# Fourteen matmuls on stored weights per turn, in front of six TensorE stages of a fused transformer kernel

## The reference, cut to what matters

```python
h = h + _L0_attn_ref(_layernorm(h), ...)   # 12 heads of 16, quantised q, k, v, weights; no softmax
h = h + _L0_ffn_ref(_layernorm(h), ...)    # routing of 41 tokens to attention, the others to a mix; then GELU, 192 -> 768 -> 192
h = h + _L1_attn_ref(_layernorm(h), ...)   # 12 heads of 16, softmax
h = h + _L1_ffn_ref(_layernorm(h), ...)    # 1 shared and 3 routed experts, 192 -> 384 -> 192
```

## Time and profile before

| | |
|---|---|
| median of 3 runs | 4890.29 us (4887.49 to 4894.54) |
| profiled execution, its own time | 4889.78 us |
| its span in the trace | 4888.1 us |
| mean granted TensorE clock | 0.871 |
| PE busy | 4106.4 us (84%), 27744 matmul instructions |
| PEld, DVE, ACT, POOL busy | 65%, 54%, 36%, 8% |

### The profile page before, as it was taken

How to read it: one execution, slowest core, us unless ns; L and a number is a source line. 1 busy time by engine, 2 the same in 40 slices (tenths; PEclk the granted TensorE clock), 3 DMA queues, 4 the chain that set the end, 5 groups by cost and what they waited for, 6 DMA issues and landing times.

```text
span 4888.1 us, 70094 instructions
## 1 busy us (share of the span) xinstructions
PE 4106.4 (84%) x27744; PEld 3173.8 (65%) x27744; DVE 2643.1 (54%) x7217; ACT 1747.0 (36%) x2774; POOL 398.9 (8%) x523
## 2 busy tenths in 40 slices
PE   2678888888888888888888888888888888888888
PEld 1556666666666666666666666666666666666666
DVE  2346555555555555555555555555555555556443
ACT  1223333433333333333334333333333343333332
POOL 2100000000000000000000000000000000000000
PEclk8668898888889988899888889888889899889888
DMA  4011111011111111111101111101111101111000
GB/s 112 23 29 34 26 35 29 27 30 32 26 35 32 30 25 30 29 32 32 32 24 30 35 26 32 32 24 29 36 26 32 32 24 33 32 26 19 13 13 4
DMA packets 154046, 147.13 MB, mean 30 GB/s; under 512 B 64359, under 2 KB 132026, under 8 KB 153722
## 3 DMA queue, kind: packets, MB, share of 16 engines
q1 hardware_dynamic: 153722, 142.64, 13.4%
HBM read 87.28 MB, written 7.91 MB: 19 GB/s over the span
## 4 chain that ended last, share of the span: by engine, by line
PE 58%; DVE 19%; SPq 5%; POOL 5%; ACT 5%; issue 5%; DMA 4%; DVEq 0%; POOLq 0%; ACTq 0%
PE area_n L1031 12%; PE area_m L1031 9%; PE area_a L1023 9%; PE area_b L1023 5%; SPq L451 5%; PE area_n L1248 4%; DMA k1s<-scratch 3%; DVE xn L730 3%; DVE mx L927 2%; PE area_n L1055 2%; PE area_a L1106 2%; PE area_m L1198 2%; ACT pT_both L655 2%; DVE part L744 2%; PE area_a L1031 1%
## 5 line engine op out<-in xcount | busy, mean ns | idle before, releaser
L927 DVE TENSOR_REDUCE mx<-area_n 91x1 f32<-91x273 f32 x1152 | 467.0, 432 | 361.1 <-PE area_n L1248 356.5
L1031 PE MATMUL area_n<-w_dn,hid 128*91 128x192 f32 x2304 | 476.4, 370 | 68.9 <-DVE mrow L932 33.5
L1023 PE MATMUL area_a<-xT,w_gu 96*128 96x273 f32 x1536 | 442.5, 435 | 68.9 <-ACT pa L600 52.4
L1031 PEld LDWEIGHTS area_n<-w_dn,hid 128*91 128x91 f32 x2304 | 411.6, 184 | 117.4 <-issue 87.2
L1248 PE MATMUL area_n<-k1s,q1s 96*91 96x273 bf16 x1152 | 349.1, 353 | 146.8 <-DMA k1s<-scratch 98.5
L1023 PEld LDWEIGHTS area_a<-xT,w_gu 96*128 96x128 f32 x1536 | 312.3, 211 | 175.8 <-ACT pa L600 62.7
L1023 PE MATMUL area_b<-xT,w_gu 96*128 96x273 f32 x1536 | 387.8, 395 | 0.0
L600 ACT ACTIVATE pa<-area_a,scal 91x820 bf16<-91x820 f32 x192 | 180.0, 938 | 544.1 <-PE area_a L1106 492.1
L1248 PEld LDWEIGHTS area_n<-k1s,q1s 96*91 96x91 bf16 x1152 | 144.4, 139 | 287.7 <-DVE mx L927 131.3
L1023 PEld LDWEIGHTS area_b<-xT,w_gu 96*128 96x128 f32 x1536 | 287.8, 191 | 59.7 <-issue 0.3
L990 DVE SCALAR_TENSOR_TENSOR outb<-area_n,cwt,outb 91x192 f32<-91x192 f32 x288 | 102.0, 407 | 396.0 <-PE area_n L1031 396.0
(11 more groups left out here) (242 smaller groups left out, 7550.3 us busy)
## 6 DMA issues: line engine op xcount, KB each, us to landing
img<-in_x SPq DMA_DIRECT2D x192, 392.0 KB, 3.5
q1s<-scratch SPq DMA_DIRECT2D x192, 102.4 KB, 3.5
k1s<-scratch SPq DMA_DIRECT2D x192, 102.4 KB, 4.3
out<-outb SPq DMA_DIRECT2D x32, 204.8 KB
q0s<-scratch SPq DMA_DIRECT2D x128, 25.6 KB, 3.3
k0s<-scratch SPq DMA_DIRECT2D x128, 25.6 KB, 2.0
pooled<-pooled_dram SPq DMA_DIRECT2D x128, 9.2 KB
tokens<-in_txt SPq DMA_DIRECT2D x32, 57.8 KB
```

What stands on the lines that cost most here:

```text
L927: v.tensor_reduce(mx[:, k:k + 1], N[0:TC, k % 2, 0:T], AX.X, ALU.max)\
L1023: last = mm(area[x][0:rows_, j, 0:n], w(j, kc), rhs[:, kc, 0:n], start=(kc == 0), stop=(kc == NK - 1))
L1031: last = mm(by_token(x)[:, c, :], lhs(i, c), w_, start=(i == 0), stop=(i == len(w) - 1))
```

## The change

In front of six stages of a turn TensorE gets extra matmuls on the down weights of the experts, 14 in all. Each has 128 x 128 numbers of `w_dn` as its stationary operand and 192 columns of it as the moving one, in float32, so that it is two instructions. They write to the area that the stage is about to write (begun as the stage begins it), with `start=True, stop=True`, and the stage's own matmuls overwrite the results; nothing reads them and no counter is raised. They stand ahead of the stage's own waits on operands, and behind the wait for its area. The order of the stages is unchanged, and no other engine's program is.

```diff
+FILL = {"mx.23": 2, "a0.0": 1, "n5f": 2, "mx.18": 4, "gt": 3, "mx.32": 2}
...
+                def fill(stage, name, k):
+
+                    x, bank = areas(stage)[0], 0
+                    if name in ("pv", "mx"):
+                        bank = k % 2
+                        t.begin_bank(x, stage, name)
+                    elif name == "pw":
+                        t.begin_bank(x, stage, "ob")
+                    else:
+                        bank = int(name == "ob")
+                        t.begin(x, stage)
+                    for i in range(FILL[stage]):
+                        mm(area[x][:, bank, 0:D], w_dn[:, i % NEXP, 0, 0:128], w_dn[:, i % NEXP, 1, :], start=True, stop=True)
+
                 for stage in t.stages:
                     name, _, k = stage.partition(".")
                     k = int(k or 0)
                     n = t.image(stage)
                     x = pair_of(name, k)
+                    if stage in FILL:
+                        fill(stage, name, k)
                     if name == "tok":
```

## The result

The changed kernel is slower. Its median is 4960.86 us over 4 runs (4952.31 to 4976.85), that of the kernel before in the same comparison 4889.99 us (4887.49 to 4894.54). The ratio is 1.0145, with a 95% interval of 1.0125 to 1.0164. The forecast of 4851 us had the wrong sign, and the result lies above its range. The profiled execution of after took 4976.85 us, the longest of the four, with a span of 4975.1 us; that of before had 4888.1.

The account below looks back on a forecast made before the run. The prediction took TensorE's own work, partly at half clock, as the bound. Costs 2.24 less gains 2.26 and 1.2 gave -1.2 us a turn, -39 us over 32 turns: 4851 us, range 4765 to 4930 us.

Parts of the forecast that it names:

- delay only what TensorE does next: All fourteen fills: they give the other engines nothing to do; costs together 2.24 us a turn.
- a0.0: Fill at a0.0, with no wait before it: cost 0.34 us a turn.
- n5f: Fill at n5f, partly in its own wait: dy.3 0.2 us late, cost 0.2 us a turn, at most 0.47.
- The turns all become long ones: Rival: n5f's fill delays mx.0 by 0.2 us, turning short turns long; 35 us, 4925 us with no gain at dy.1; chance 0.24.
- C: Low-clock stretch with s1.1 and ey.4: the clock no longer falls there, giving back 2.26 us a turn.
- gt: Fill at gt, 1.02 us, fits into the wait for ScalarE's copy before a0.2: cost 0.
- mx.18: Fill at mx.18, 1.36 us, partly absorbed by two shrinking waits: cost 0.6 us a turn, ends 0.5 and 0.9.
- mx.23: Fill at mx.23, 0.68 us, partly absorbed by t1.1's wait: cost 0.5 us a turn, ends 0.34 and 0.68.
- D: Low-clock stretch behind c1, slowing dy.1: gain between nothing and 2.4 us a turn, half taken, 1.2 us.
- mx.32: Fill at mx.32, 0.68 us, before a 0.30 us wait: cost 0.6 us a turn, 0.4 at full clock, 0.9 at half.
- Nothing arrives: Rival: the 2.26 us gained meet 2.24 us of fills and the clock still falls behind c1; 4890 us; chance 0.13.
- The size of a fill: Each fill instruction of 192 columns takes 0.17 us at full clock, upper bound 0.25; one filling matmul 0.34 us.

Follow-up runs that it names:

- e8_a00_n5f: The kernel before with only the fills at a0.0 (1) and n5f (2): 4969.5 us, ratio 1.0162.
- e1_gt_mx18: The kernel before with only the fills at gt (3) and mx.18 (4): 4867.2 us, ratio 0.9957.
- e4_only_n5f: The kernel before with only the two fills at n5f: 4909.4 us, ratio 1.0034.
- e15_four: The changed kernel without the fills at a0.0 and n5f, leaving mx.23, mx.18, gt and mx.32: 4877.0 us, ratio 0.9969.
- e13_behind_rta: The changed kernel with two more fills behind rta, in front of a0.1: 4963.3 us, ratio 1.0140 to the kernel before.
- e14_b_c_a01: e11_b_c with its two fills at a0.1, behind rta, instead of ahead of rta: 4840.4 us, ratio 0.9895 to the kernel before.
- e9_a00: The kernel before with only the one fill at a0.0: 4926.1 us, ratio 1.0064.
- e5_mx0: e1_gt_mx18 with six more fills in front of mx.0: 4864.4 us, ratio 0.9950 to the kernel before.
- e11_b_c: The kernel before with fills at gt (3), mx.18 (4), mx.0 (6), gate (2) and rta (2): 4772.6 us, ratio 0.9752.
- e2_no_a00: The changed kernel without the fill at a0.0: 4917.6 us, ratio 1.0050 to the kernel before.
- e3_no_n5f: The changed kernel without the fills at n5f: 4925.1 us, ratio 1.0069 to the kernel before.
- e16_no_rta: e11_b_c without the fills at rta: 4825.7 us, ratio 0.9861 to the kernel before.

## Why the prediction was wrong

**The step that failed** is the sentence that the fills "delay only what TensorE does next", and with it the costs of `a0.0` (0.34) and `n5f` (0.2). As lengths they were nearly right: 0.33 and 0.30 us arrive. As costs they were far too small. e8_a00_n5f has these two alone and its turn is 2.91 us longer than before, not 0.54. Held against the clock's rise in `v0`, `rta` comes 0.45 to 0.7 us later than before (6.34 to 7.21 us, 5.89 to 6.49 before). In the turns in which it comes 6.79 us or later the clock falls during `dy.0`, which costs 4.84 - 3.16 = 1.68 us there and 3.52 - 2.01 = 1.51 in `ey.3`; over the 28 turns of after that is a mean of 0.90 and 0.84 us. The rest of the excess lies around `v1`, where the late fall of the short turns became the early one of the long turns in most cases.

The prediction read the places at which the clock already fell and asked what the fills would do there. It did not ask which stretches had so far just held it. `rta`, 1.9 us of mostly one-column matmuls behind a wait of 0.82 us, was one: it stood inside the band given at e1_gt_mx18 in all 28 turns of before, and its rows were not looked at.

**The rival with the right side.** "The turns all become long ones" named the mechanism for `n5f` and sized it at 35 us. e4_only_n5f shows that `n5f` alone does that for 0.34%, 17 us: the 28 turns go from 17 to 21 slow `v1`, not to 28. The change as a whole passed 4925 us because of the fall at `dy.0`, which no rival had.

**C, right.** Forecast 2.26 us a turn. `s1.1` went from 2.03 to 1.10 and `ey.4` from a mean of 3.25 to 2.01: 0.93 + 1.24 = 2.17 us, in every turn, in every kernel with wide fills at both places. The 52.8 us of waits became 22.8 (forecast "some 20"). `gt` cost nothing, as forecast: its six instructions take 1.18 us and `a0.2` still waits 0.79. From `s1.0` to `c1` e1_gt_mx18 is 17.73 - 16.26 = 1.47 us shorter, so that `mx.18` cost 2.17 - 1.47 = 0.7 (forecast 0.6). e15_four has 0.66 us less gain there, which is `mx.23` (forecast 0.5).

**D, wrong.** Half of 2.4 us was entered as a gain, and 0.27 came. The fall stayed, in after and in e15_four alike; `dy.1` went from 5.41 to 5.14 us in after and not at all in e15_four (5.40). And `mx.32`'s fill runs at half the clock: 1.52 us for four instructions in the timeline above, where `mx.23`'s take 0.81. From `c1` to `dy.1` the turn is 0.80 us longer, against a forecast of 0.6. So between `s1.0` and `dy.1` the change gives 0.81 and takes 0.80: what C brings net is handed back before `dy.1`. This is what the rival "Nothing arrives" said, and if only these four fills had been added the prediction would have been right in sign, with 4877 us for its 4851, but by luck: most of the gain of e15_four lies around `v1`, where the prediction expected nothing.

**The size of a fill.** Eight instructions take 1.47 us and four take 0.81 at the full clock, 0.165 us more for each; 0.17 was taken.

**The sum, corrected.** Costs 0.7 + 0.66 + 0.8 + 0.33 + 0.30 = 2.79, gain 2.17, so +0.62; with `dy.1` -0.27 it is +0.35. The new low clock is `dy.0` and `ey.3` 0.90 + 0.84 = 1.74 and the other 0.88 around `v1` (1.21 - 0.33), together 2.62. That makes 2.97 us a turn, measured 2.95; 32 x 2.95 = 94 us, where the spans differ by 87; the mean is of 28 turns, and the others, some with stages missing, were not taken apart.

**The clock going up and down.** The trace of before already showed the clock going down and up several times in a turn. The Trainium skill, "TensorE: Matmul & The Clock Gate", section "A second HAM failure mode: psum-queue depth-cycling", has a kernel whose many short idle times between groups of matmuls make the clock go to and fro. The trace agrees at C, where TensorE was busy for 1.69 of 3.4 us ahead of the fall. At `rta` it does not bear the rule out: there it counts as busy for 3.36 of 3.40 us ahead of the fall in e8_a00_n5f. The same page of the Trainium skill, section "What's actually happening", says that the gate keeps a time of its own which does not start with the kernel. That a shift of 0.3 us without any new wait decides about `dy.0` would fit it, which is argued; no run here shows the gate's own time.

**What stays open.** Why the clock holds with `rta` inside that band and falls on either side of it is not shown; the band is read from the traces, and no run was made to move `rta` by itself. Why the fills behind `rta` raised the number of slow `dy.0` (15 to 21 in e13_behind_rta, 24 in e14_b_c_a01) is not explained: they make `rta`'s followers denser and yet did harm. That the place of `v1` in the gate's own time makes a turn long is argued from the classes of turn lengths, not shown. Moving stages so that `rta` or `c1` lie among dense ones was not tried.

## What to carry to other kernels

- Where TensorE's clock goes up and down within a loop, a matmul of 0.3 us that no wait covers can cost several times itself (e9_a00: 31 us for 11 us of work), since it moves thin stretches that have so far just held the clock. List those stretches too, not only the ones at which the clock falls.
- Put filling matmuls only into waits that stay waits, make them wide, and fill all the thin places that follow each other before judging one: e5_mx0 gained nothing on e1_gt_mx18, and with two more places filled e11_b_c gained 2%.
- Test each place by itself and in pairs. e4 and e9 add up to 0.98%, their pair costs 1.62%.

## What the runs showed of the hardware

- Wide instructions held the clock at C and narrow ones did not: with 18 of one column `s1.1` stayed at 2.03 us, with 14 of 192 columns it took 1.10.
- The clock falls without an idle TensorE. In after and in e8_a00_n5f it went from 1.00 and 0.99 to about 0.5 behind a stretch that is busy for 3.30 and 3.36 of 3.40 us, in 35 instructions.
- In before, after, e2_no_a00, e3_no_n5f, e9_a00 and e15_four the lengths of turns stand in classes, near 143.4, 146.7 and 150.2 us with next to nothing between, so that a small change of work moves turns from one class to the next. In the other kernels there are others as well, near 141.1 and 145.4 us in e1_gt_mx18 and e16_no_rta, near 141.1 and 142.2 in e11_b_c.
- Whether the clock falls at the thin stretch `rta` went with where that lies after the clock's last rise: `dy.0` is fast in every turn in which `rta` starts 5.86 to 6.75 us after the rise in `v0`, slow up to 5.82 and from 6.77 on, in thirteen kernels.
- At half the clock a fill costs nearly twice: 1.52 us for four instructions against 0.81.
